# Cross attention: x behind it turned by VectorE and passed through DRAM, its linear one slot later and behind the queries

## The chip, the cores and the metric

One core of one Trainium2 chip runs the whole program. The metric is the time of one execution on the device in microseconds (us), lower is better. Engines are called TensorE (PE; its loads of weights PEld), VectorE (DVE), ScalarE (ACT), GpSimd (POOL) and SyncE (SP), as in the profile.

## The reference

Two transformer layers on x of 4 x 1024 x 512 in float32. The first layer is a state-space mixer, a cross attention and a tanh of three linears; the second is a windowed attention, a strided cross attention and a feed-forward on 4-bit values. Each is added to x and normalised. The stage that matters here is the middle of the first layer:

```python
qh = (q @ Wq.T + bq).reshape(B, S, H, D_K).transpose(0, 2, 1, 3)
scores = jnp.einsum('bhqd,bhkd->bhqk', qh, kh) / np.sqrt(D_K)
scores = jnp.where(mask, scores, -1000000000.0)
weights = jax.nn.softmax(scores, axis=-1)
out = jnp.einsum('bhqk,bhkd->bhqd', weights, vh)
...
return out @ Wo.T + bo                  # x = layernorm(x + this)
...
h = jnp.einsum('btc,cd->btd', x, weight)
h = jnp.einsum('btc,cd->btd', h, aux_weight1)
h = jnp.einsum('btc,cd->btd', h, aux_weight2)
return jnp.tanh(h + bias)               # x = layernorm(x + this)
```

There are 16 heads of 32 and 64 keys. The three linears have no non-linearity between them and are folded to one matrix `WF` in the stage before; keys and values are laid out there too (`KBD`, `VBD`).

## The kernel before

Five stages run one after the other: constants, the mixer with products of weights, `cross_attention_and_linears` (the one that changes), local attention, and the rest with the feed-forward. x stays in SBUF all the time, as 32 tiles of 128 tokens by 512 (`NT = 32`); tile n is of batch n % 4 and group n // 4.

The stage is a software pipeline written out by hand. Every engine walks the same list of slots, `SLOTS`, from -8 on, and in slot s does its part for several tiles; engines meet only by semaphores, each engine doing its own list strictly in order. In slot s TensorE does, in this order: transposes of x of tile s + 8 (`transpose_x`, four, L954), transposes of the softmax weights of tile s - 2 (`transpose_p`, eight, L994), a `query` product for four tiles at a time (L977, a product a slot, so until slot 27), `weigh` of tile s - 2 (L1002, weights times values), transposes of the normalised x2 of tile s - 3 (`transpose_x2`, four, again L954), `scores` of tile s (L986), `project` of tile s - 2 (L1012) and `linear` of tile s - 3 (L1022). In float32 each 128x512 matmul stands as two instructions in the trace.

VectorE does in slot s: `biased` (the linear's product plus its bias, L1131), `total` of the last slot's exponentials and their reciprocal (L1102, L1105), `added` (x plus the tanh, and its statistics, L1136), `masked` (scores times the mask, out of PSUM, L1090), the normalisation of the layer behind (L1119), `shifted` (maximum and subtraction, L1096 and L1098), `attended` (x plus the projection, L1125, and its statistics) and its normalisation. Between `masked` and `shifted` GpSimd adds the mask's fill (`hide`, L921). ScalarE copies the transposes out of PSUM (L1052, L1057, L1074, L1079), evicts the query (L1069), and does exp (L1082) and tanh (L1061). GpSimd also scales by the reciprocals (L926), adds a bias to x (L932) and takes the inverse roots (L939, L948).

The three products of a slot share two PSUM banks in turn:

```python
turn = lambda n, i: 5 + (3 * n + i) % 2
```

So a product may start only when the product two before it has been taken out of its bank. Before the change the order is query, project, linear: `query` follows on the bank of the last slot's `project` and waits for its sum, `s_a2`, i.e. `attended`; `project` follows on the last slot's `linear` and waits for `s_lbd`, i.e. `biased`; `linear` follows on this slot's `query` and waits for `s_qe`.

Of the kernel before, what the change touches and what calls it, by code (L numbers as in the profile page):

```python
# [13 lines left out]
P = 128  # L14
B = 4
# [43 lines left out]
class Kernel:  # L59
    def __init__(self, nc, ctx, a, out):  # L60
# [18 lines left out]
        self.GTd, self.AOd = self.dram("unit_gT", (B * C, P, T)), self.dram("attended", (P, B * C, T))  # L79
        self.YD = self.dram("half_log_norm", (B, 3 * H, T), BF16)  # L80
# [769 lines left out]
def cross_attention_and_linears(k):  # L850
# [6 lines left out]
    with ExitStack() as ctx:  # L857
# [26 lines left out]

        turn = lambda n, i: 5 + (3 * n + i) % 2
# [4 lines left out]
        SLOTS = range(-2 * B, NT + 5)  # L890

        with k.nc.Block() as block:
            @block.sync
            def _(e):
# [3 lines left out]
                for t, n in ((bo, "L0_xattn_bo"), (lb, "L0_ffn_bias")):  # L898
                    e.dma_start(t[:, :], rows_of(a[n])).then_inc(s_lb.sem, 16)

# [4 lines left out]
                e.dma_start(bg[:, :], rows_of(a["L1_attn_bg"])).then_inc(s_next.sem, 16)  # L905
                e.wait_ge(s_next.sem, s_next.at(48))

            @block.gpsimd
            def _(e):
# [24 lines left out]
                for s in SLOTS:  # L934
                    if there(s - 1):
                        weights(s - 1)
                    if there(s - 4):
                        e.wait_ge(s_v3.sem, s_v3.at(s - 3))
                        e.tensor_tensor(rs3[:, :], ve3[:, :], k.mhalf[:, 0:1], ALU.pow).then_inc(s_r3.sem, 1)  # L939
# [11 lines left out]
            def _(e):  # L951
# [5 lines left out]
                def transpose_x(n):  # L957
                    e.wait_ge(s_xe.sem, s_xe.at(n - 11))
# [4 lines left out]
                def transpose_x2(n):  # L963
                    e.wait_ge(s_x2.sem, s_x2.at(n + 1))
                    e.wait_ge(s_tc.sem, s_tc.at(min(n + 12, NT)))
                    e.wait_ge(s_xe.sem, s_xe.at(n))
                    transposed(XTB, x_tile(n), s_xl)

                def query(i):
# [5 lines left out]
                    e.wait_ge(s_a2.sem, s_a2.at(s - 2))  # L975
# [30 lines left out]
                def project(n):  # L1006
# [3 lines left out]
                    e.wait_ge(s_lbd.sem, s_lbd.at(n - 1))  # L1010
                    for c in range(C):
                        mm = e.matmul(bank[turn(s, 1)][:, :], AT[:, c, :], WoT[:, c, :], start=(c == 0), stop=(c == C - 1))  # L1012
                    mm.then_inc(s_o.sem, 1)

                def linear(n):
                    s = n + 3
                    e.wait_ge(s_xe.sem, s_xe.at(n + 1))

                    e.wait_ge(s_qe.sem, s_qe.at(min(s + B + 1, NT)))
                    e.wait_ge(s_a2.sem, s_a2.at(min(n, NT)))  # L1020
                    for c in range(C):
                        mm = e.matmul(bank[turn(s, 2)][:, :], XL[:, c, :], WF[:, c, :], start=(c == 0), stop=(c == C - 1))  # L1022
                    mm.then_inc(s_l.sem, 1)

                for s in SLOTS:
# [4 lines left out]
                    if there(s + B):  # L1030
                        query(s + B)
                    if there(s - 2):
                        weigh(s - 2)
                    if there(s - 3):
# [5 lines left out]
                    if there(s - 3):  # L1040
                        linear(s - 3)

            @block.scalar
            def _(e):
                four = lambda x: x.rearrange("p (n t) -> p n t", n=C)

                for s in SLOTS:
# [10 lines left out]
                    if there(s - 4):  # L1058
                        n = s - 4
                        e.wait_ge(s_lbd.sem, s_lbd.at(n + 1))  # L1060
                        e.activation(TH[:, :], TH[:, :], ACT.Tanh).then_inc(s_th.sem, 1)  # L1061
# [13 lines left out]
                    if there(s - 3):  # L1075
                        n = s - 3
                        e.wait_ge(s_xl.sem, s_xl.at(n + 1))
                        e.wait_ge(s_l.sem, s_l.at(n))
                        e.activation(XL[:, :, :], four(bank[XTB][:, :]), ACT.Copy).then_inc(s_xe.sem, 1)  # L1079
                    if there(s):  # L1080
                        e.wait_ge(s_sx.sem, s_sx.at(s + 1))
                        e.activation(SM[s % RS][:, :], SM[s % RS][:, :], ACT.Exp).then_inc(s_e.sem, 1)  # L1082

            @block.vector
            def _(e):
# [35 lines left out]
                def attended(n):  # L1121
# [3 lines left out]
                    e.tensor_tensor(y, bank[turn(n + 2, 1)][:, :], y, ALU.add).then_inc(s_a2.sem, 1)  # L1125
                    statistics(n, y, st2, mv2, ve2, s_a2, s_t2, s_m2, s_v2, s_r2)

                def biased(n):
                    e.wait_ge(s_l.sem, s_l.at(n + 1))
                    e.wait_ge(s_a3.sem, s_a3.at(n))  # L1130
                    e.tensor_tensor(TH[:, :], bank[turn(n + 3, 2)][:, :], lb[:, :], ALU.add).then_inc(s_lbd.sem, 1)  # L1131
# [6 lines left out]

                e.wait_ge(s_bq.sem, s_bq.at(16))
                e.tensor_scalar(bqs[:, :], bq[:, :], SC, None, ALU.mult).then_inc(s_bqs.sem, 1)  # L1140
                e.wait_ge(s_lb.sem, s_lb.at(32))
                for s in SLOTS:
                    if there(s - 4):
                        biased(s - 4)
                    if there(s - 1):
                        total(s - 1)
                    if there(s - 4):
# [1374 lines left out]
```

## Time and profile before

| | us |
|---|---|
| median of the runs shown | 2681.29 (2680.92 to 2684.01) |
| the profiled execution | 2683.64 |
| its span, first to last instruction | 2681.8 |
| mean granted clock of TensorE | 0.988 |
| TensorE, VectorE, GpSimd, ScalarE busy | 2556.6, 1915.6, 866.7, 749.1 |
| this stage's first `masked` to its last instruction | 420.3 to 906.7 |

In the profile a row of the timeline has the start, the duration, the engine, the line, the operation and in brackets the idle time before it with what ended it. Matmuls one behind the other are merged to one row with their count. "PEclk" is the granted share of TensorE's clock, 1.00 being 2.4 GHz and 0.50 being 1.2 GHz. Issues of DMAs stand under the queue that issues them (SPq, ACTq).

### The profile page before, as it was taken

Reading aid. Unit: us, or ns where it says so; the run is one execution under the profiler, and the core shown is the slowest. Engines: PE = TensorE matmul, PEld = TensorE weight load, DVE = VectorE, ACT = ScalarE, POOL = GpSimd, SP = SyncE. Lnnn points to the kernel's source line nnn. Section 1 sums busy time; section 2 is a strip of 40 time slices with the busy share of each in tenths; the row PEclk is TensorE's granted clock in tenths of the full one; section 3 lists DMA queues with packets and bytes.
Section 4 is the critical chain, followed back from the end, with each engine's and each line's share of the span. In section 5 each row is a group of like instructions: output and inputs, shape, how many; then the busy total and the mean of one; then the engine's idle time right before and its main releaser. Section 6 shows DMA issues by size and latency. Waiting matters only on the chain. (4 is left out here: it accounts for less than half of the span.)

```text
span 2681.8 us, 36822 instructions
## 1 busy us (share of the span) xinstructions
PE 2556.6 (95%) x13053; PEld 1575.2 (59%) x13053; DVE 1915.6 (71%) x3262; ACT 749.1 (28%) x1103; POOL 866.7 (32%) x900
## 2 busy tenths in 40 slices
PE   8999998999999898999988879999999999999998
PEld 4444544555555444454544447777777777777775
DVE  4788403666667436777778858888888888888886
ACT  1111223333332235666668621111110111111100
POOL 2222203555455346676767711111111111111000
PEclk9999999999999999999999979999999999999999
DMA  5444130000000143343444421111111111111111
GB/s 175 146 151 171 52 98 35 1 0 1 1 1 1 33 103 98 98 103 95 106 105 134 139 95 36 45 45 45 46 46 44 46 43 43 43 43 46 38 39 36
DMA packets 269604, 175.94 MB, mean 66 GB/s; under 512 B 104912, under 2 KB 235344, under 8 KB 268399
## 3 DMA queue, kind: packets, MB, share of 16 engines
q1 hardware_dynamic: 238742, 148.59, 19.3%
q10 hardware_dynamic: 30680, 24.98, 3.3%
q8 instruction: 107, 1.75, 0.3%
q14 instruction: 75, 0.61, 0.1%
HBM read 90.51 MB, written 52.43 MB: 53 GB/s over the span
## 5 line engine op out<-in xcount | busy, mean ns | idle before, releaser
L2099 PE MATMUL bank<-tiles,tl_XQT 128*128 128x512 f32 (+1 forms) x768 | 328.1, 570 | 0.8 <-issue 0.8
L2104 PE MATMUL bank<-tiles,tl_XQT 128*128 128x512 f32 (+1 forms) x768 | 317.9, 557 | 0.0
L2116 PE MATMUL bank<-tiles,tl_HT 128*128 128x512 f32 x682 | 304.2, 602 | 5.0 <-DMA tl_HT<-tl_tmp 5.0
L2099 PEld LDWEIGHTS bank<-tiles,tl_XQT 128*128 128x128 f32 x768 | 233.5, 310 | 72.6 <-issue 15.8
L2104 PEld LDWEIGHTS bank<-tiles,tl_XQT 128*128 128x128 f32 x768 | 236.7, 308 | 65.9 <-issue 0.5
L2116 PEld LDWEIGHTS bank<-tiles,tl_HT 128*128 128x128 f32 x682 | 219.2, 324 | 75.7 <-issue 10.9
L1403 POOL TENSOR_SCALAR_AFFINE_SELECT tiles<-tiles 128x512 f32<-128x512 f32 x256 | 182.7, 716 | 170.1 <-ACT tiles L1630 154.4
L2179 ACT ACTIVATE tl_HQ<-bank 128x512 f32<-128x512 f32 (+1 forms) x96 | 53.9, 562 | 580.4 <-PE bank L2099 545.7
L2046 POOL TENSOR_TENSOR tl_rs<-tl_ve,mhalf 128x1 f32<-128x1 f32 x29 | 15.9, 548 | 537.1 <-DVE tl_ve L2258 537.1
L1730 DVE SCALAR_TENSOR_TENSOR tiles<-tiles,bank 128x1024 f32<-128x1024 f32 (+1 forms) x128 | 141.7, 1148 | 18.8 <-PE bank L1506 18.7
L1408 POOL TENSOR_SCALAR_AFFINE_SELECT tiles<-tiles 128x512 f32<-128x512 f32 x224 | 152.6, 681 | 0.0
L2038 POOL TENSOR_TENSOR tl_rs<-tl_ve,mhalf 128x1 f32<-128x1 f32 x32 | 18.7, 584 | 402.0 <-DVE tl_ve L2240 402.0
L1630 ACT ACTIVATE tiles<-bank 128x1024 f32<-128x1024 f32 (+1 forms) x128 | 123.4, 964 | 28.2 <-PE bank L1465 28.1
L1635 ACT ACTIVATE tiles<-tiles 128x1024 f32<-128x1024 f32 (+1 forms) x128 | 124.8, 1000 | 20.0 <-DVE tiles L1730 17.0
L1555 PE MATMUL bank<-home_T,tiles 128*128 128x512 f32 x256 | 121.5, 619 | 3.5 <-ACT tiles L1664 0.9
L977 PE MATMUL bank<-space_T 128*128 128x512 f32 x256 | 118.6, 607 | 2.5 <-DVE X L1125 2.3
L1567 PE MATMUL bank<-home_odd,tiles 128*128 128x512 f32 x256 | 117.4, 601 | 0.0
L1022 PE MATMUL bank<-space_T,space_quant 128*128 128x512 f32 x256 | 115.2, 593 | 1.5 <-ACT space_quant L1079 1.5
L1012 PE MATMUL bank<-space_even,space_quant 128*128 128x512 f32 x256 | 115.3, 593 | 1.2 <-ACT space_quant L1074 1.1
L1428 POOL TENSOR_TENSOR la_rn<-la_n,mhalf 128x16 f32<-128x16 f32 x32 | 92.7, 2897 | 52.2 <-DVE la_n L1805 52.2
L2054 PE MATMUL bank<-home_T,attended_values 128*128 128x512 f32 x232 | 107.1, 605 | 0.0
L921 POOL TENSOR_TENSOR xl_SM<-xl_SM,xl_nm 128x1024 f32<-128x1024 f32 x32 | 80.0, 2499 | 78.8 <-DVE xl_SM L1090 78.8
(301 smaller groups left out, 4701.3 us busy)
## 6 DMA issues: line engine op xcount, KB each, us to landing
tl_HT<-tl_tmp SPq DMA_DIRECT2D x248, 44.0 KB, 2.0
tl_HT<-tl_tmp ACTq DMA_DIRECT2D x248, 44.0 KB, 2.0
fp_weights<-space_quant ACTq DMA_DIRECT2D x33, 256.0 KB, 2.5
X<-in_x SPq DMA_DIRECT2D x8, 1024.0 KB, 10.7
v<-tiles SPq DMA_DIRECT2D x32, 256.0 KB, 2.4
unit_g<-tiles SPq DMA_DIRECT2D x32, 256.0 KB, 2.4
unit_gT<-tiles SPq DMA_DIRECT2D x128, 64.0 KB, 2.1
la_GN<-unit_g SPq DMA_DIRECT2D x128, 64.0 KB, 2.0
```

The costliest lines, as they stand in the source:

```text
L977: mm = e.matmul(bank[turn(s, 0)][:, :], WqT[:, c, m * P:(m + 1) * P], XT[g % 2][:, c, :], start=(c == 0), stop=(c == C - 1))
L1012: mm = e.matmul(bank[turn(s, 1)][:, :], AT[:, c, :], WoT[:, c, :], start=(c == 0), stop=(c == C - 1))
L1403: return e.affine_select(out=x[:, :, 0:P], in_=x[:, :, 0:P], compare_op=ALU.is_ge, fill=fill, base=0, pattern=[[0, HC], [1, P]], channel_m ...
L1408: return e.affine_select(out=x[:, :, P:WIN], in_=x[:, :, P:WIN], compare_op=ALU.is_ge, fill=fill, base=0, pattern=[[0, HC], [-1, P]], chan ...
L1555: mm = e.matmul(bank[1][:, :], XT[m % 2][:, c, :], WgT[:, c, :], start=(c == 0), stop=(c == C - 1))
L1567: mm = e.matmul(bank[2][:, :], XT[m % 2][:, c, :], WvT[:, c, :], start=(c == 0), stop=(c == C - 1))
L1630: e.activation(TR[p % RING][:, :, 0:cols(t)], four(ARG[:, :])[:, :, 0:cols(t)], ACT.Tanh).then_inc(s_T.sem, 1)
L1635: e.activation(y, y, ACT.Exp).then_inc(s_p.sem, 1)
L1730: e.scalar_tensor_tensor(out=y, in0=y, scalar=1.0, in1=d, op0=ALU.add, op1=ALU.mult).then_inc(s_u.sem, 1)
L2099: mm = e.matmul(bank[(2 * q) % 3][:, 0:w], chunk(XQT[n % 2], c), WgT[q][:, :, c, :], start=(c == 0), stop=(c == C - 1))
L2104: mm = e.matmul(bank[(2 * q + 1) % 3][:, 0:w], chunk(XQT[n % 2], c), WuT[q][:, :, c, :], start=(c == 0), stop=(c == C - 1))
L2116: mm = e.matmul(bank[DOWN][:, :], chunk(HT, q), WdT[:, q, :], start=(q == 0), stop=(q == IC - 1))
```

## The change

The x2 that the linear reads is no longer turned by TensorE and copied out by ScalarE. VectorE turns it in blocks of 32x32 into one of two new tiles, `XB2`, behind the normalisation (`x2_turned`). In the next slot SyncE stores the four quarters of it to DRAM in four DMAs, each putting its blocks in place, and ScalarE's queue loads the whole back in one DMA, into the tile `XL`, whose columns now lie token by token with the four chunks side by side. The last two tiles keep TensorE's transposes. The `linear` of a tile runs one slot later than before, and within its slot behind `query` instead of at the end; `biased` stays with the same tile's slot number s - 4 but moves behind `shifted`, `added` and its normalisation go one slot later, and tanh moves behind exp. The order of the three products in the shared banks is now query, linear, project, and each waits accordingly: `query` for `biased` of the slot before, `linear` for `attended` of the slot before, `project` for this slot's `query`. There is one slot more at the end.

```diff
+        self.X2d = self.dram("x2_turned", (2, P, D))
...
-        SLOTS = range(-2 * B, NT + 5)
+        SLOTS = range(-2 * B, NT + 6)
...
+        by_blocks = lambda n: 0 <= n < NT - 2
+        XB2 = [sb(f"XB2{n}", [P, D]) for n in range(2)]
+        XLT = XL[:, :, :].rearrange("p c t -> p (c t)")
+        in_chunks = lambda x: x.rearrange("p (t c) -> p c t", c=C)
+        s_tu, d_tu, d_xl = sem("x2_turned"), [sem(f"x2_stored{n}") for n in range(2)], sem("x2T_load")
...
+                def x2_stored(n):
+                    e.wait_ge(s_tu.sem, s_tu.at(n + 1))
+                    e.wait_ge(d_xl.sem, d_xl.at(16 * (n - 1)))
+                    for i in range(4):
+                        e.dma_start(k.X2d[n % 2].rearrange("(j p) w -> p j w", j=4)[:, :, P * i:P * i + P],
+                                    XB2[n % 2][32 * i:32 * i + 32, :].rearrange("p (j w) -> p j w", j=4)).then_inc(d_tu[n % 2].sem, 16)
...
+                for s in SLOTS:
+                    if by_blocks(s - 3):
+                        x2_stored(s - 3)
...
-                    if there(s - 4):
-                        e.wait_ge(s_v3.sem, s_v3.at(s - 3))
+                    if there(s - 5):
+                        e.wait_ge(s_v3.sem, s_v3.at(s - 4))
                         e.tensor_tensor(rs3[:, :], ve3[:, :], k.mhalf[:, 0:1], ALU.pow).then_inc(s_r3.sem, 1)
...
                 def transpose_x(n):
-                    e.wait_ge(s_xe.sem, s_xe.at(n - 11))
                     if n > B:
...
                 def transpose_x2(n):
                     e.wait_ge(s_x2.sem, s_x2.at(n + 1))
-                    e.wait_ge(s_tc.sem, s_tc.at(min(n + 12, NT)))
-                    e.wait_ge(s_xe.sem, s_xe.at(n))
+                    e.wait_ge(s_tc.sem, s_tc.at(NT))
+                    e.wait_ge(s_xe.sem, s_xe.at(n - NT + 2))
                     transposed(XTB, x_tile(n), s_xl)
...
                     s = i - B
                     e.wait_ge(s_qe.sem, s_qe.at(i - 1))
-                    e.wait_ge(s_a2.sem, s_a2.at(s - 2))
+                    e.wait_ge(s_lbd.sem, s_lbd.at(s - 4))
...
                     s = n + 2
                     e.wait_ge(s_ae.sem, s_ae.at(n + 1))
 
+                    e.wait_ge(s_qe.sem, s_qe.at(min(s + B + 1, NT)))
+                    e.wait_ge(s_lbd.sem, s_lbd.at(n - 2))
+                    for c in range(C):
+                        mm = e.matmul(bank[turn(s, 2)][:, :], AT[:, c, :], WoT[:, c, :], start=(c == 0), stop=(c == C - 1))
+                    mm.then_inc(s_o.sem, 1)
+                def linear(n):
+                    s = n + 4
+                    if by_blocks(n):
+                        e.wait_ge(d_xl.sem, d_xl.at(16 * (n + 1)))
+                    else:
+                        e.wait_ge(s_xe.sem, s_xe.at(n - NT + 3))
+                    e.wait_ge(s_a2.sem, s_a2.at(min(s - 2, NT)))
                     e.wait_ge(s_lbd.sem, s_lbd.at(n - 1))
                     for c in range(C):
-                        mm = e.matmul(bank[turn(s, 1)][:, :], AT[:, c, :], WoT[:, c, :], start=(c == 0), stop=(c == C - 1))
-                    mm.then_inc(s_o.sem, 1)
-
-                def linear(n):
-                    s = n + 3
-                    e.wait_ge(s_xe.sem, s_xe.at(n + 1))
-
-                    e.wait_ge(s_qe.sem, s_qe.at(min(s + B + 1, NT)))
-                    e.wait_ge(s_a2.sem, s_a2.at(min(n, NT)))
-                    for c in range(C):
-                        mm = e.matmul(bank[turn(s, 2)][:, :], XL[:, c, :], WF[:, c, :], start=(c == 0), stop=(c == C - 1))
+                        mm = e.matmul(bank[turn(s, 1)][:, :], in_chunks(XLT)[:, c, :], WF[:, c, :], start=(c == 0), stop=(c == C - 1))
                     mm.then_inc(s_l.sem, 1)
 
                 for s in SLOTS:
@@ -1029,16 +1053,16 @@
                         transpose_p(s - 2)
                     if there(s + B):
                         query(s + B)
+                    if there(s - 4):
+                        linear(s - 4)
                     if there(s - 2):
                         weigh(s - 2)
-                    if there(s - 3):
+                    if there(s - 3) and not by_blocks(s - 3):
                         transpose_x2(s - 3)
                     if there(s):
                         scores(s)
                     if there(s - 2):
                         project(s - 2)
-                    if there(s - 3):
-                        linear(s - 3)
 
             @block.scalar
             def _(e):
@@ -1055,10 +1079,6 @@
                         e.wait_ge(s_pt.sem, s_pt.at(n + 1))
                         e.wait_ge(s_at.sem, s_at.at(n))
                         e.activation(PT[:, :, :], PTB.rearrange("p (n t) -> p n t", n=H // 2), ACT.Copy).then_inc(s_pe.sem, 1)
-                    if there(s - 4):
-                        n = s - 4
-                        e.wait_ge(s_lbd.sem, s_lbd.at(n + 1))
-                        e.activation(TH[:, :], TH[:, :], ACT.Tanh).then_inc(s_th.sem, 1)
                     if there(s + B):
                         i = s + B
                         g, m = i // C, i % C
@@ -1072,14 +1092,23 @@
                         e.wait_ge(s_at.sem, s_at.at(n + 1))
                         e.wait_ge(s_o.sem, s_o.at(n))
                         e.activation(AT[:, :, :], four(bank[AB][:, :]), ACT.Copy).then_inc(s_ae.sem, 1)
-                    if there(s - 3):
+                    if by_blocks(s - 3):
                         n = s - 3
-                        e.wait_ge(s_xl.sem, s_xl.at(n + 1))
+                        e.wait_ge(d_tu[n % 2].sem, d_tu[n % 2].at(64 * (n // 2 + 1)))
                         e.wait_ge(s_l.sem, s_l.at(n))
-                        e.activation(XL[:, :, :], four(bank[XTB][:, :]), ACT.Copy).then_inc(s_xe.sem, 1)
+                        e.dma_start(XLT, k.X2d[n % 2]).then_inc(d_xl.sem, 16)
+                    elif there(s - 3):
+                        n = s - 3
+                        e.wait_ge(s_xl.sem, s_xl.at(n - NT + 3))
+                        e.wait_ge(s_l.sem, s_l.at(n))
+                        e.activation(in_chunks(XLT), four(bank[XTB][:, :]), ACT.Copy).then_inc(s_xe.sem, 1)
                     if there(s):
                         e.wait_ge(s_sx.sem, s_sx.at(s + 1))
                         e.activation(SM[s % RS][:, :], SM[s % RS][:, :], ACT.Exp).then_inc(s_e.sem, 1)
+                    if there(s - 4):
+                        n = s - 4
+                        e.wait_ge(s_lbd.sem, s_lbd.at(n + 1))
+                        e.activation(TH[:, :], TH[:, :], ACT.Tanh).then_inc(s_th.sem, 1)
 
             @block.vector
             def _(e):
@@ -1122,13 +1151,13 @@
                     y = x_tile(n)
                     e.wait_ge(s_o.sem, s_o.at(n + 1))
                     e.wait_ge(s_xb.sem, s_xb.at(n + 1))
-                    e.tensor_tensor(y, bank[turn(n + 2, 1)][:, :], y, ALU.add).then_inc(s_a2.sem, 1)
+                    e.tensor_tensor(y, bank[turn(n + 2, 2)][:, :], y, ALU.add).then_inc(s_a2.sem, 1)
                     statistics(n, y, st2, mv2, ve2, s_a2, s_t2, s_m2, s_v2, s_r2)
 
                 def biased(n):
                     e.wait_ge(s_l.sem, s_l.at(n + 1))
                     e.wait_ge(s_a3.sem, s_a3.at(n))
-                    e.tensor_tensor(TH[:, :], bank[turn(n + 3, 2)][:, :], lb[:, :], ALU.add).then_inc(s_lbd.sem, 1)
+                    e.tensor_tensor(TH[:, :], bank[turn(n + 4, 1)][:, :], lb[:, :], ALU.add).then_inc(s_lbd.sem, 1)
 
                 def added(n):
                     y = x_tile(n)
@@ -1136,25 +1165,32 @@
                     e.tensor_tensor(y, TH[:, :], y, ALU.add).then_inc(s_a3.sem, 1)
                     statistics(n, y, st3, mv3, ve3, s_a3, s_t3, s_m3, s_v3, s_r3)
 
+                def x2_turned(n):
+                    e.wait_ge(s_x2.sem, s_x2.at(n + 1))
+                    e.wait_ge(d_tu[n % 2].sem, d_tu[n % 2].at(64 * (n // 2)))
+                    e.transpose(XB2[n % 2][:, :].rearrange("p (j r c) -> p c j r", j=4, r=32), x_tile(n)).then_inc(s_tu.sem, 1)
                 e.wait_ge(s_bq.sem, s_bq.at(16))
                 e.tensor_scalar(bqs[:, :], bq[:, :], SC, None, ALU.mult).then_inc(s_bqs.sem, 1)
                 e.wait_ge(s_lb.sem, s_lb.at(32))
                 for s in SLOTS:
+                    if there(s - 1):
+                        total(s - 1)
+                    if there(s - 5):
+                        added(s - 5)
+                    if there(s):
+                        masked(s)
+                    if there(s - 5):
+                        normal(s - 5, mv3, rs3, s_r3, s_x3)
+                    if there(s):
+                        shifted(s)
                     if there(s - 4):
                         biased(s - 4)
-                    if there(s - 1):
-                        total(s - 1)
-                    if there(s - 4):
-                        added(s - 4)
-                    if there(s):
-                        masked(s)
-                    if there(s - 4):
-                        normal(s - 4, mv3, rs3, s_r3, s_x3)
-                    if there(s):
-                        shifted(s)
                     if there(s - 2):
                         attended(s - 2)
                         normal(s - 2, mv2, rs2, s_r2, s_x2)
+                    if by_blocks(s - 2):
+                        x2_turned(s - 2)
 
 
 FULL = P + 1
```

## Rows read from the trace of the kernel before

**Rows 1.** The page's part 1: busy us and share of the span, instructions.
```profile
PE 2556.6 (95%) x13053; PEld 1575.2 (59%) x13053; DVE 1915.6 (71%) x3262; ACT 749.1 (28%) x1103; POOL 866.7 (32%) x900
```

**Rows 2.** Windows, a stretch mid-stage: us, busy of each engine, PEclk, DMA share, GB/s.
```profile
634.00:691.00 57.00, 57.00 (x244) 32.70 (x241) 36.68 (x61) 19.01 (x27) 29.59 (x22) 1.00 0.00 1
```

**Rows 3.** Timeline of one steady slot: start us, us, engine, line, operation, count, [idle before].
```profile
651.51 3.60 PE L1012 MATMUL bank<-space_even,space_quant 128*128 128x512 f32 x8
...
651.72 1.23 DVE L1090 TENSOR_TENSOR xl_SM<-bank,xl_mf 128x1024 f32<-128x1024 f32 x1 [1.93 <-PE bank L986]
...
654.95 3.60 PE L1022 MATMUL bank<-space_T,space_quant 128*128 128x512 f32 x8
...
658.03 0.68 DVE L1125 TENSOR_TENSOR X<-bank,X 128x512 f32<-128x512 f32 x1
...
658.38 0.60 PE L954 MATMUL bank<-ident,X 128*128 128x128 f32 x4
...
659.69 3.60 PE L977 MATMUL bank<-space_T 128*128 128x512 f32 x8
...
663.22 1.09 PE L1002 MATMUL bank<-xl_PT,space_quant 128*64 128x128 f32 x16
...
664.25 0.66 PE L954 MATMUL bank<-ident,X 128*128 128x128 f32 x4
...
664.74 1.89 PE L986 MATMUL bank<-space_quant,space_T 128*128 128x256 f32 x8
...
666.67 1.23 DVE L1090 TENSOR_TENSOR xl_SM<-bank,xl_mf 128x1024 f32<-128x1024 f32 x1 [1.91 <-PE bank L986]
```

**Rows 4.** Timeline of the third slot.
```profile
445.27 1.04 PE L994 MATMUL bank<-ident,xl_SM 128*128 128x128 f32 x8
...
447.75 0.68 DVE L1125 TENSOR_TENSOR X<-bank,X 128x512 f32<-128x512 f32 x1
...
448.58 5.37 PE L977 MATMUL bank<-space_T 128*128 128x512 f32 x8 [2.27 <-DVE X L1125]
...
449.30 1.02 ACT L1057 ACTIVATE xl_PT<-bank 128x1024 f32<-128x1024 f32 x1
...
457.32 1.23 DVE L1090 TENSOR_TENSOR xl_SM<-bank,xl_mf 128x1024 f32<-128x1024 f32 x1 [5.11 <-PE bank L986]
```

**Rows 5.** Line L1090 in slots 26 and 27: op, count, ns min/median/max, starts.
```profile
L1090 DVE TENSOR_TENSOR xl_SM<-bank,xl_mf x2: 1224/1224/1225, 799.9 to 814.4; 128x1024 f32<-128x1024 f32 x2
```

**Rows 6.** Timeline: the last `masked`, and the stage's last VectorE instruction.
```profile
867.07 1.23 DVE L1090 TENSOR_TENSOR xl_SM<-bank,xl_mf 128x1024 f32<-128x1024 f32 x1
...
906.10 0.55 DVE L1119 TENSOR_SCALAR X<-X,xl_mv,xl_rs 128x512 f32<-128x512 f32 x1 [0.66 <-POOL xl_rs L939]
```

**Rows 7.** Windows of 2 us behind the waits of rows 4 and 8.
```profile
450.00:452.00 2.00, 2.00 (x4) 0.93 (x3) 1.71 (x3) 0.32 (x1) 0.21 (x1) 0.50 0.00 0
850.00:852.00 2.00, 2.00 (x14) 1.67 (x12) 1.97 (x4) 1.17 (x3) 0.00 (x1) 0.50 0.00 0
874.00:876.00 2.00, 0.45 (x9) 0.41 (x10) 1.17 (x4) 1.54 (x2) 0.43 (x1) 1.00 0.00 0
```

**Rows 8.** Timeline of TensorE: two waits of the last slots.
```profile
849.01 1.85 PE L1002 MATMUL bank<-xl_PT,space_quant 128*64 128x128 f32 x16 [1.92 <-ACT xl_PT L1057]
...
873.01 1.04 PE L994 MATMUL bank<-ident,xl_SM 128*128 128x128 f32 x8
...
875.60 1.09 PE L1002 MATMUL bank<-xl_PT,space_quant 128*64 128x128 f32 x16 [1.55 <-ACT xl_PT L1057]
```

**Rows 9.** Line L2381, a transpose on VectorE: count, ns min/median/max, starts.
```profile
L2381 DVE STREAM_TRANSPOSE tl_QB<-tl_XQ x31: 1082/1109/1166, 1594.2 to 2618.8; 128x512 f32<-128x512 f32 x31
```

**Rows 10.** The page's part 6: DMA issues, count, KB each, us to landing.
```profile
tl_HT<-tl_tmp SPq DMA_DIRECT2D x248, 44.0 KB, 2.0
...
fp_weights<-space_quant ACTq DMA_DIRECT2D x33, 256.0 KB, 2.5
X<-in_x SPq DMA_DIRECT2D x8, 1024.0 KB, 10.7
```

## The prediction

> **What bounds the kernel now.** I read the page's busy times first: TensorE works 95% of the span [rows 1], so a change pays only where it shortens TensorE's stream or its waits. The windows of the stage come next: in the middle of the cross attention TensorE is busy for all of 57 us, while VectorE has 36.68 and ScalarE 19.01 [rows 2]. The time order of one slot then gives the order that the stage lives by [rows 3]. I count a slot from one `masked` (VectorE, L1090) to the next: 651.72 to 666.67, 14.95 us. The reader should see two things. VectorE, which runs `masked` to the end of `attended`'s sum (658.03 + 0.68 = 658.71), holds a PSUM bank that the next `query` needs; `query` starts at 659.69, so today this comes 0.83 us early, allowing the 0.15 us that lay between such a sum's end and the query elsewhere (448.43 to 448.58 [rows 4]). And it comes early only because TensorE has two products of 3.44 us, `project` and `linear`, to do between `scores` and `query`.
>
> The same time order at the third slot [rows 4] is the one place where that cover is missing: there is no `linear` yet, and `query` waits 2.27 us for the sum of L1125. The whole argument rests on this row.
>
> **The change, part by part.** *Removed:* four transposes of x2 per tile, 30 times. From L954's start at 664.25 to `scores` at 664.74 is 0.49 us [rows 3]. A TensorE that never waited would need 14.95 - 0.49 = 14.46 us a slot. The copy on ScalarE goes too, worth nothing, since ScalarE has a third of the work.
>
> *Moved:* `linear`, one slot later, from behind `project` to behind `query`. Its bank is now emptied by `biased`, which VectorE reaches only behind `masked` and `shifted` of that slot; and `query` of the next slot waits for exactly that `biased` (`s_lbd.at(s - 4)`). Now only `project` and twelve transposes lie between `scores` and `query`, as in rows 4. So a ring closes: scores, masked, hide on GpSimd, max, subtraction, biased, query, linear, weigh, scores. It is worked out with steady rows:
> - `masked` to the end of the sum, which `biased` replaces at the same shape: 651.72 to 658.71, 6.99 us [rows 3]; `hide` on GpSimd is inside it.
> - to `query`: 0.15 us [rows 4].
> - `query` to `weigh`, today adjacent: 659.69 to 663.22, 3.53 us; `linear` between them adds 651.51 to 654.95, 3.44 us [rows 3].
> - `weigh` to what follows it: 663.22 to 664.25, 1.03 us; `scores` to `masked`: 664.74 to 666.67, 1.93 us [rows 3].
>
> Sum 17.07 us a slot. Behind the waiting `query` stand linear, weigh, scores and project, in that order, so everything waits. TensorE would stand still 17.07 - 14.46 = 2.6 us in each slot.
>
> Which slots? `query` is there up to slot 27 and its wait means something from slot 5 on. Step by step:
> - *Slots 3 and 4 gain.* `query` of slot 3 no longer waits for `attended`. It would start near 446.3, when the eight transposes of P end (445.27 + 1.04 [rows 4]); `weigh` then waits for the copy of P^T (449.30 + 1.02 = 450.32 [rows 4]) and starts at 450.45, so masked(3) is at 450.45 + 1.03 + 1.93 = 453.4 instead of 457.32. masked(4) follows 14.46 later, at 467.9, instead of 457.32 + 14.95 = 472.3. Gain 4.4 us.
> - *Slots 5 to 27:* 23 x 17.07 = 392.6, so masked(27) at 860.5 instead of 814.4 [rows 5]: 46.1 us late.
> - *Slots 28 to 31* have no `query`. There `linear` waits for `attended`, which is one sum further on (0.68 + 0.03): 6.99 + 0.71 + 0.15 + 3.53 + 1.03 + 1.93 = 14.34 a slot, 57.4 in all, so masked(31) at 917.9 instead of 867.07 [rows 6]: 50.8 us late.
> - *The drain* from masked(31) to the stage's last instruction takes 906.10 + 0.55 - 867.07 = 39.6 us [rows 6]. One slot is added, but the slots are short there. Following VectorE through slots 32 to 36 with the same durations I get 41.6: 2.0 more.
>
> Sum 52.8 us without any effect on the clock.
>
> *The clock.* Where TensorE waited 2.27 us, the clock then fell to 0.50, which is the 1.2 GHz level (450 to 452 [rows 7]), and the query took 5.37 instead of 3.60 us, 1.77 more [rows 3, 4]. After a wait of 1.92 us it fell too, after one of 1.55 us it did not [rows 7, 8]. Here each of 27 slots has such a wait, of 2.6 us or more. From below this costs 0, from above 27 x 1.77 = 48 us. I take one in three for the 23 waits of 2.6 us, nearer to never, since they are only a little above the one that cost nothing, and all four in slots 28 to 31, where a sum more (0.71) comes before `linear` and four transposes fewer before the wait, so that it is about 3.5 us: 12 x 1.77 = 21 us.
>
> There is a rule that bears on this. The Trainium skill, page "TensorE: Matmul & The Clock Gate", section "Part 4: PE-mode transpose", says that transposes do not count as activity for the clock the way matmuls do. By that rule the twelve transposes and the wait behind them would be one long pause, and the clock would fall in every slot. The trace bears it out only by half: after eight transposes and 1.55 us of waiting the clock was still at 1.00 [rows 7, 8]. It is rival 2 below.
>
> *Added on VectorE:* 30 transposes of 128x512, 1.11 us each at the nearest row, which also writes with a stride [rows 9]. VectorE stands idle 1.91 us before `masked` now [rows 3], so its own round is 14.95 - 1.91 = 13.04, and becomes 14.2 us. That lies beside a ring of 17.07: nothing. If the cover went (TensorE at 14.46) it would still just fit; in slots 28 to 31 it equals the ring, and I count nothing.
>
> *Added DMAs:* four stores of 64 KB on SP's queue, one load of 256 KB on ScalarE's. A transfer out of a turned tile lands after 2.0 us, a 256 KB one after 2.5 [rows 10]; the upper bound is 10.7 us, that of 1 MB. SP has only the next stage's weights ahead of them, issued at the stage's start. The turned tile is ready at the latest when VectorE's round ends, 14.2 us after `masked`; four stores one after another, 2.0 each, are there by 22.2, and the load behind them by 24.7. ScalarE is free for it before that: it gets there behind `weigh` of the next slot, at 17.07 - 1.93 = 15.1 and a copy. `linear` needs it two slots on, at 34.14 - 1.93 - 1.03 - 3.53 = 27.7. Three us of slack by upper bounds: nothing. Behind the issue on ScalarE stand exp and tanh; exp of that slot waits for `shifted` anyway, until 17.07 + 6.3 = 23.4, so a load issued by then holds up nothing.
>
> *Other edits at nothing:* tanh behind exp (its reader `added` is a slot's start later); `transpose_x` without its wait; the stationary operand read in steps of four elements, since a load of weights has a 512-column product to hide behind. The later `added` costs only the drain, counted above.
>
> **The sum.** 52.8 + 21 = 74 us on the profiled execution of 2683.6, whose span is 2681.8. That execution is 2.35 above the median of the runs, 2681.3, so I forecast 2755.
>
> **The rivals.**
> 1. *The ring without the clock.* For it: between waits TensorE works ten us and more at a stretch, and 1.55 us did no harm. Against: two of two longer ones did. 2681.3 + 52.8 = 2734.
> 2. *The clock falls in every slot.* 2681.3 + 52.8 + 48 = 2782. For it: the row of rows 4 is the same order of work. Against: a fall lengthens the slot, so the next wait meets other work before it.
> 3. *The bank is free in time and TensorE stays the bound* (the other side). This holds from the point where masked-to-biased takes less than project and twelve transposes, 3.44 + 1.31 (658.38 to 659.69 [rows 3]) = 4.75 instead of 7.1 us. Then -4.4, 19 slots at 14.46 and 4 at 14.0 (no more x to turn ahead) against 342.1 give -15.7 by slot 27, VectorE's 14.2 in the last four gives +4.6, the drain +2: -9, so 2672. Against: all durations on that path are measured, and none of its instructions goes.
> 4. *The transfers are late.* If stores and load took 10.7 us each, the turned x would be there at 14.2 + 10.7 + 10.7 = 35.6 instead of 27.7, 7.9 late over two slots, so 4 a slot: 23 x 4 = 92 more than the forecast, 2847. Against: this stage leaves the DMA engines idle (their share is 0.00 in [rows 2]).
>
> **How the numbers follow.** Forecast, the ring with a clock that falls in some slots: 0.58. Rival 1: 0.18. Rival 2: 0.16. Rival 3: 0.05. Rival 4: 0.03. The range takes in the first three with a few us for a ring that is 0.2 us a slot shorter or longer: 2729 to 2789. About 0.2% (5 us) is what a measurement can tell from no change. Faster is rival 3, 0.05; same 0.02, a partial form of it; slower 0.93.
>
> **What would show it.** In the changed trace: `masked` to `masked` near 17.1 us or 18.8, not 14.95; TensorE waiting some 2.5 us before `query`, released by VectorE's `biased`, 23 times; the granted clock at 0.50 after some of these; no wait at `linear` for the load; VectorE still idle before `masked`. I am wrong if `query` starts straight behind the transposes of P, or if `linear` waits for a DMA.

## The result: slower by 2.5%, by a ring through the queries' bank

| | before | changed |
|---|---|---|
| median, us | 2681.51 | 2750.16 (2749.24 to 2753.03) |
| ratio | | 1.0254, 95% interval 1.0239 to 1.0268 |
| span of the profiled execution | 2681.8 | 2749.3 |
| last instruction of the stage on VectorE ends at | 906.65 | 974.22 |

The ratios here and below are of fast runs alone; one execution of e6 (9374.67 us) and one of the kernel before beside it (10908.97 us) are slow ones and are left out.

The forecast was 2755. The stage ends 67.6 us later, the span is 67.5 longer, so all of it is in this stage. On the page TensorE's busy time has hardly moved against [rows 1] (2556.6), only its share of a longer span; and the group of the queries (line, shapes, count, busy and mean ns, then the idle time before them and what ended it) names the loss:

```profile
PE 2557.7 (93%) x12933; PEld 1595.3 (58%) x12933; DVE 1944.9 (71%) x3292; ACT 728.0 (26%) x1073; POOL 866.3 (32%) x900
...
L997 PE MATMUL bank<-space_T 128*128 128x512 f32 x256 | 123.6, 628 | 57.7 <-DVE xl_TH L1160 57.7
```

One steady slot of the changed kernel in order of time, to be laid beside [rows 3]:

```profile
643.77 1.23 DVE L1119 TENSOR_TENSOR xl_SM<-bank,xl_mf 128x1024 f32<-128x1024 f32 x1 [3.17 <-PE bank L1006]
...
650.09 0.68 DVE L1160 TENSOR_TENSOR xl_TH<-bank,xl_lb 128x512 f32<-128x512 f32 x1
...
650.91 3.67 PE L997 MATMUL bank<-space_T 128*128 128x512 f32 x8 [2.44 <-DVE xl_TH L1160]
...
653.75 1.11 DVE L1171 STREAM_TRANSPOSE xl_XB<-X 128x512 f32<-128x512 f32 x1
...
654.42 3.60 PE L1046 MATMUL bank<-space_T,space_quant 128*128 128x512 f32 x8
...
657.95 1.09 PE L1022 MATMUL bank<-xl_PT,space_quant 128*64 128x128 f32 x16
...
658.98 1.99 PE L1006 MATMUL bank<-space_quant,space_T 128*128 128x256 f32 x8
...
661.01 1.23 DVE L1119 TENSOR_TENSOR xl_SM<-bank,xl_mf 128x1024 f32<-128x1024 f32 x1 [3.18 <-PE bank L1006]
```

The reader should see the ring closing: `masked` (L1119) at 643.77, `biased` (L1160) behind `shifted`, `query` (L997) 0.14 us after `biased` ends and 2.44 us late, then `linear`, `weigh`, `scores`, and `masked` again at 661.01: 17.24 us, against 14.95. VectorE is no bound, since it idles 3.18 us before `masked`.

### The profile page after: what moved, and what is told of

Its sections match the earlier page's. It is cut to its first block and busy times, and to the rows that moved or that the text cites. A ratio compares the mean times of both kernels' runs of the same rounds, so it can differ in the third digit from the quotient of the medians.

```text
span 2749.3 us, 36735 instructions
## 1 busy us (share of the span) xinstructions
PE 2557.7 (93%) x12933; PEld 1595.3 (58%) x12933; DVE 1944.9 (71%) x3292; ACT 728.0 (26%) x1073; POOL 866.3 (32%) x900
## 5 line engine op out<-in xcount | busy, mean ns | idle before, releaser
L997 PE MATMUL bank<-space_T 128*128 128x512 f32 x256 | 123.6, 628 | 57.7 <-DVE xl_TH L1160 57.7
L1046 PE MATMUL bank<-space_T,space_quant 128*128 128x512 f32 x256 | 121.8, 620 | 19.1 <-issue 18.0
L1119 DVE TENSOR_TENSOR xl_SM<-bank,xl_mf 128x1024 f32<-128x1024 f32 x32 | 39.1, 1223 | 112.6 <-PE bank L1006 112.6
L997 PEld LDWEIGHTS bank<-space_T 128*128 128x128 f32 x256 | 48.5, 200 | 112.4 <-issue 112.1
```

Of the source, the lines that this page charges most:

```text
L997: mm = e.matmul(bank[turn(s, 0)][:, :], WqT[:, c, m * P:(m + 1) * P], XT[g % 2][:, c, :], start=(c == 0), stop=(c == C - 1))
L1046: mm = e.matmul(bank[turn(s, 1)][:, :], in_chunks(XLT)[:, c, :], WF[:, c, :], start=(c == 0), stop=(c == C - 1))
```

## The experiments

Each run shows the edit against the changed kernel. Line numbers in the text are the changed kernel's; in the rows they are those of the run. "A slot" is from one `masked` to the next; its number is that of the tile that `masked` then takes, and slots are measured from the starts of that line in the profiled execution. "The drain" is from the last `masked`, masked(31), to the stage's last instruction on VectorE. "A fall" is a stretch in which the granted clock of TensorE is 0.50 (1.2 GHz) instead of 1.00. "VectorE's round" is the time from one `masked` to the next when `masked` does not wait for `scores`: VectorE's own work and its waits for GpSimd. Rival A holds VectorE's transposes to be the cost, rival B the passage through DRAM.

**e1, `biased` ahead of `masked`.**

```diff
                     if there(s - 5):
                         added(s - 5)
+                    if there(s - 4):
+                        biased(s - 4)
                     if there(s):
                         masked(s)
...
-                    if there(s - 4):
-                        biased(s - 4)
```

> The changed kernel with one thing put back: VectorE takes `biased` of tile s - 4 ahead of `masked` instead of behind `shifted`. Theory (the ring through `biased`): `query` finds its bank empty, the wait of 2.44 us before it goes 23 times, a slot is TensorE's own stream, 14.5 us instead of 17.24, and the whole kernel comes to 2674 us (2670 to 2680), below the kernel before. Rival A (VectorE's transposes are the cost): a slot stays above 15 us, 2690 or more, and VectorE has no idle time before `masked`. Rival B (the passage through DRAM is late): `linear` waits instead of `query`, and the time stays near 2750.

Measured 2682.97, ratio to the kernel before 0.9996 (0.9987 to 1.0005): no difference from before, and 67 us below the changed kernel. In the timeline of e1 the query follows the transposes without a wait:

```profile
642.68 1.22 DVE L1119 TENSOR_TENSOR xl_SM<-bank,xl_mf 128x1024 f32<-128x1024 f32 x1 [0.47 <-PE bank L1006]
...
646.35 1.04 PE L1014 MATMUL bank<-ident,xl_SM 128*128 128x128 f32 x8
...
647.23 3.60 PE L997 MATMUL bank<-space_T 128*128 128x512 f32 x8
...
657.25 1.22 DVE L1119 TENSOR_TENSOR xl_SM<-bank,xl_mf 128x1024 f32<-128x1024 f32 x1 [0.44 <-PE bank L1006]
```

A slot is 14.56 us and masked(27) comes at 801.1, 13.3 us earlier than in the kernel before. So the cause is shown: this one position costs the whole loss. But I had forecast 2674, and 11.9 of the 13.3 us were lost again behind it: slots 28 to 31 took 61.8 us (before: 52.6) and the drain 42.3 (39.6). In slot 29, where the clock did not fall, the slot is 13.99 us, VectorE's round; the other three are 15.45, 15.57 and 16.83, so of the 9.2 us lost there 5.9 are falls. The profiled execution is the slowest of the eleven of e1 (2684.69; the fastest, 2674.71, had a mean granted clock of 0.989 instead of 0.985), so not every execution loses as much. `linear` waits for `attended` in these slots, by its semaphore and by the times (L1154 ends 0.11 us before it), and the clock falls behind the wait:

```profile
852.43 0.68 DVE L1154 TENSOR_TENSOR X<-bank,X 128x512 f32<-128x512 f32 x1
853.22 6.75 PE L1046 MATMUL bank<-space_T,space_quant 128*128 128x512 f32 x8 [2.83 <-issue]
```

**e2, the order alone,** x2 turned by TensorE and copied by ScalarE as before.

```diff
-        by_blocks = lambda n: 0 <= n < NT - 2
+        by_blocks = lambda n: False
...
                 def transpose_x(n):
+                    e.wait_ge(s_xe.sem, s_xe.at(n - 11))
...
-                    e.wait_ge(s_tc.sem, s_tc.at(NT))
-                    e.wait_ge(s_xe.sem, s_xe.at(n - NT + 2))
+                    e.wait_ge(s_tc.sem, s_tc.at(min(n + 12, NT)))
+                    e.wait_ge(s_xe.sem, s_xe.at(n))
...
```

> The changed kernel's order on all engines, but x2 turned by TensorE and copied by ScalarE for all tiles, with no transpose on VectorE and no new DMA. Theory (the ring): the loss is all there, and the four transposes between `weigh` and `scores` lie inside the ring: 17.24 + 0.49 = 17.73 us a slot, 2763 us in all (2755 to 2785, by how often the clock falls). Rivals A and B (VectorE's transposes, the passage through DRAM): without them the time comes back to 2681 or at least below 2700.

Measured 2773.75, ratio 1.0338 (1.0324 to 1.0352). The loss is there without a transpose on VectorE or a new DMA, so rivals A and B are out. Two queries in the timeline of e2 show the same wait as above and a slot of 17.63 us. That is 0.1 less than the 17.73 expected: with the transposes of x2 ahead of it again, `scores` to `masked` takes 1.93 us (612.75 to 614.68) and not the changed kernel's 2.03:

```profile
604.20 3.67 PE L998 MATMUL bank<-space_T 128*128 128x512 f32 x8 [2.45 <-DVE xl_TH L1161]
...
621.83 3.67 PE L998 MATMUL bank<-space_T 128*128 128x512 f32 x8 [2.44 <-DVE xl_TH L1161]
```

It is slower than my 2763 because the clock fell in 9 of slots 5 to 27 (5, 8, 11 and so on to 26, and 27); more on that below.

**e3, the turning alone,** with the products in the old order (query, project, linear).

```diff
                 def query(i):
-                    e.wait_ge(s_lbd.sem, s_lbd.at(s - 4))
+                    e.wait_ge(s_a2.sem, s_a2.at(s - 2))
...
-                    if there(s - 4):
-                        linear(s - 4)
                     if there(s - 2):
                         weigh(s - 2)
...
                         project(s - 2)
+                    if there(s - 4):
+                        linear(s - 4)
...
                 for s in SLOTS:
+                    if there(s - 5):
+                        biased(s - 5)
                     if there(s - 1):
                         total(s - 1)
```

> The other half alone: x2 turned by VectorE and passed through DRAM, its linear one slot later, but the products in the order of the kernel before (query, project, linear at the slot's end) with its waits, `biased` at the head of VectorE's slot, tanh where it was; the load stands behind exp on ScalarE's queue. Theory (the ring): two products lie again between `scores` and `query`, which waits for `attended` and finds it done; 14.5 us a slot while x is still turned ahead, 14.1 to 14.3 in the last slots where VectorE's round bounds: 2676 us (2671 to 2682). Rivals A and B: 2700 and more, since everything that they blame is in it.

Measured 2683.63, ratio 1.0003 (0.9994 to 1.0012). The rivals' "2700 and more" is wrong, the ring's middle is right (14.56 us a slot), and my 2676 is too low for the same reason as in e1: from its first `masked` to masked(27) it is 10.7 us faster than before, but the last four slots take 56.5 us, 14.12 each, which is VectorE's round with the transpose, and the drain 47.0, since `linear` is a slot later and at that slot's end. I had booked next to nothing for either.

**e4, no transpose, no store, no load.** `x2_turned`, `x2_stored` and the load are not called, nor waited for.

> The changed kernel without VectorE's 30 transposes, the 120 stores and the 30 loads; the linear of tiles 0 to 29 multiplies whatever lies in its tile, so the values of x are not the reference's from there on, the work of all other instructions being the same. Theory (the ring): none of them is in the ring, a slot stays 17.24 us and the time 2750 (2740 to 2758). Rivals A and B: the time falls by 30 us or more.

Measured 2753.97, ratio 1.0264 (1.0249 to 1.0278), as the ring has it. The wait in its timeline is the same:

```profile
641.83 1.23 DVE L1114 TENSOR_TENSOR xl_SM<-bank,xl_mf 128x1024 f32<-128x1024 f32 x1 [4.20 <-PE bank L1005]
...
648.98 3.67 PE L996 MATMUL bank<-space_T 128*128 128x512 f32 x8 [2.44 <-DVE xl_TH L1155]
...
659.07 1.23 DVE L1114 TENSOR_TENSOR xl_SM<-bank,xl_mf 128x1024 f32<-128x1024 f32 x1 [4.20 <-PE bank L1005]
```

The slot is 17.24 and VectorE's idle time before `masked` grows by 1.03 us, from 3.17 to 4.20: in slots 5 to 27 the transpose had lain in it. In the last four slots e4 is no clean comparison: they took 67.4 us, 6.1 more than in the changed kernel, since behind nearly the same wait as there (3.38 us, 3.43 in the changed kernel) the clock stayed low for longer and `linear` took 6.45 us instead of 3.60:

```profile
891.41 6.45 PE L1043 MATMUL bank<-space_T,space_quant 128*128 128x512 f32 x8 [3.38 <-DVE X L1149]
```

**e5, the ring cut at the fill.**

```diff
                     e.wait_ge(s_mk.sem, s_mk.at(n + 1))
-                    e.tensor_tensor(x, x, nm[(n // B) % 2][:, n % B, :].unsqueeze(1).to_broadcast([P, H, S2]), ALU.add).then_inc(s_hid.sem, 1)
+                    e.wait_ge(s_hid.sem, s_hid.at(n))
+                    e.memset(none[:, :], 0.0).then_inc(s_hid.sem, 1)
...
                 def shifted(n):
-                    e.wait_ge(s_hid.sem, s_hid.at(n + 1))
+                    e.wait_ge(s_mk.sem, s_mk.at(n + 1))
```

> The changed kernel with the ring cut at another member: GpSimd no longer adds the mask's fill (`hide` is a memset of one column), and `shifted` waits for `masked` alone; masked scores are 0 and not -1e9, so the values differ from the reference's. The fill takes the time between the layer normalisation behind `masked` and the maximum, 645.45 to 647.69 in the changed kernel's steady slot, 2.2 us. Theory (the ring): a slot is 17.24 - 2.2 = 15.04, some 0.5 us above TensorE's own 14.56, the wait before `query` shrinks from 2.44 to 0.3, the clock no longer falls there, and the whole comes to 2685 us (2678 to 2693). Rival (the ring is not what bounds, GpSimd's fill being hidden): 2745 or more.

Measured 2671.98, ratio to the kernel before 0.9963 (0.9949 to 0.9977), 78 us below the changed kernel. In the timeline of e5 a slot is 14.91 us (15.04 expected), and TensorE is ready for the query almost when `biased` ends:

```profile
639.55 1.23 DVE L1120 TENSOR_TENSOR xl_SM<-bank,xl_mf 128x1024 f32<-128x1024 f32 x1 [3.18 <-PE bank L1007]
...
643.53 0.69 DVE L1161 TENSOR_TENSOR xl_TH<-bank,xl_lb 128x512 f32<-128x512 f32 x1
...
644.37 3.67 PE L998 MATMUL bank<-space_T 128*128 128x512 f32 x8
...
654.46 1.23 DVE L1120 TENSOR_TENSOR xl_SM<-bank,xl_mf 128x1024 f32<-128x1024 f32 x1 [3.17 <-PE bank L1007]
```

`masked` to the end of `biased` is 4.67 us (639.55 to 644.22), 7.00 in the changed kernel: 2.33 us out of the ring took 2.33 us off the slot. The total is below my 2685 because I left out the other slots. From the first `masked` to masked(4) e5 takes 4.4 us less than the changed kernel, slots 28 to 31, at 12.15 and without falls, 12.7 less, and the drain 3.8 less.

**e7 and e8, each transpose done twice,** in the changed kernel and in e1.

```diff
+                    e.transpose(XB2[n % 2][:, :].rearrange("p (j r c) -> p c j r", j=4, r=32), x_tile(n)).then_inc(s_once.sem, 1)
+                    e.wait_ge(s_once.sem, s_once.at(n + 1))
                     e.transpose(XB2[n % 2][:, :].rearrange("p (j r c) -> p c j r", j=4, r=32), x_tile(n)).then_inc(s_tu.sem, 1)
```

> The changed kernel with each of VectorE's 30 transposes done twice, 1.11 us more a slot. Theory (the ring): VectorE has 3.17 us of idle time before `masked`, so slots stay at 17.24; only the last four, at 14.48 against a round of VectorE of 14.1, could grow by 0.8 each: 2752 us (2742 to 2760). Rival A (VectorE's transposes are the cost): 30 x 1.11 = 33 more, 2783.

> The same doubling in the kernel with `biased` ahead of `masked` (e1), where a slot is 14.56 us and VectorE's idle time before `masked` 0.4. Here the cover is gone: VectorE's round of 14.1 becomes 15.25, so slots 5 to 27 grow to 15.25 and the last by 1.1: 23 x 0.7 + 4 x 1.1 = 20 more, 2703 us (2697 to 2712). If it stays at 2683, VectorE's round is shorter than I read it.

Measured 2756.5 (ratio 1.0278, 1.0261 to 1.0294) and 2700.65 (1.0070, 1.0055 to 1.0084). The same 33 us of VectorE cost some 6 us in the one, 18 in the other. In e7 the slot without a fall is still 17.24; slots 5 to 27 take 4.5 us more than in the changed kernel only by three more falls, and slots 28 to 31 2.4 more. In e8 a slot is 15.17 and `masked` no longer waits. First e7, where the 3.76 of the first row stands behind a fall and the 2.04 of the second is the steady value, then e8:

```profile
643.75 1.23 DVE L1120 TENSOR_TENSOR xl_SM<-bank,xl_mf 128x1024 f32<-128x1024 f32 x1 [3.76 <-PE bank L1007]
...
660.98 1.23 DVE L1120 TENSOR_TENSOR xl_SM<-bank,xl_mf 128x1024 f32<-128x1024 f32 x1 [2.04 <-PE bank L1007]
```

```profile
650.09 1.21 DVE L1120 TENSOR_TENSOR xl_SM<-bank,xl_mf 128x1024 f32<-128x1024 f32 x1
...
665.26 1.22 DVE L1120 TENSOR_TENSOR xl_SM<-bank,xl_mf 128x1024 f32<-128x1024 f32 x1
```

**e6, e9 and e10, the last slots mended in e1.** e6 and e9 are one kernel; e10 is the same with `LATE = 2`.

```diff
+        LATE = 6
-        by_blocks = lambda n: 0 <= n < NT - 2
+        by_blocks = lambda n: 0 <= n < NT - LATE
+        line_bank = lambda s: turn(s, 1) if s < NT - B else 5
+        proj_bank = lambda s: turn(s, 2) if s < NT - B else 6
...
                 def linear(n):
-                    e.wait_ge(s_a2.sem, s_a2.at(min(s - 2, NT)))
-                    e.wait_ge(s_lbd.sem, s_lbd.at(n - 1))
+                    if s < NT - B:
+                        e.wait_ge(s_a2.sem, s_a2.at(s - 2))
+                        e.wait_ge(s_lbd.sem, s_lbd.at(n - 1))
+                    else:
+                        e.wait_ge(s_lbd.sem, s_lbd.at(n))
```

(`project` waits for `s_a2` of tile n - 1 from slot 28 on.)

> The kernel with `biased` ahead of `masked` (e1), with two changes for its last slots, where it lost again what it had won: only tiles 0 to 25 are turned by VectorE and the last six by TensorE, and from slot 28 on, where there is no query, `linear` and `project` keep a bank each, so that neither waits for `attended` of the slot before. Theory (the last slots are bound by VectorE's round, 14.1 us with the transpose and 13.0 without, and by waits of TensorE that let the clock fall): slots 28 to 31 take 52 to 54 us instead of 61.8, the stage ends near 895 and the whole is 2673 us (2668 to 2679). Rival (the last slots are bound by TensorE and the added slot alone): no change, 2683.

> The kernel e6 once more, word for word, for a better interval of its difference from the kernel before: 2672 us (2669 to 2675), ratio 0.996.

> e6 with one of its two changes only: `linear` and `project` keep a bank each from slot 28 on, but tiles 0 to 29 are turned by VectorE as in the changed kernel. Theory (two causes in the last slots: the waits for `attended`, and VectorE's round of 14.1 with its transpose): slots 28 to 31 take 4 x 14.1 = 56.5 us, between e1's 61.8 and e6's 54.0, and the whole 2675 us (2672 to 2679). If only the waits matter it equals e6; if only VectorE's round matters it equals e1, 2683.

Measured: e6 2671.74 (without the execution left out above), ratio 0.9959 (0.9945 to 0.9973); e9 2671.87, 0.9954 (0.9940 to 0.9968); e10 2674.15, 0.9965 (0.9953 to 0.9978). All three are faster than both kernels, e9 by 0.46% than the one before: little, but no interval reaches 1. In e9's timeline slots 30 and 31 are 12.98 and 12.97 us (13.59 and 12.99 in the kernel before), and VectorE does not wait at their ends:

```profile
828.57 1.23 DVE L1127 TENSOR_TENSOR xl_SM<-bank,xl_mf 128x1024 f32<-128x1024 f32 x1 [0.99 <-PE bank L1009]
...
841.55 1.21 DVE L1127 TENSOR_TENSOR xl_SM<-bank,xl_mf 128x1024 f32<-128x1024 f32 x1
...
854.52 1.22 DVE L1127 TENSOR_TENSOR xl_SM<-bank,xl_mf 128x1024 f32<-128x1024 f32 x1
```

Slots 28 to 31 take 54.0 us in e6 and e9 and 56.0 in e10 (61.8 in e1). Most of what e1 lost there came back by the banks alone. A slot of e10 is 14.00 us, no shorter than e1's slot without a fall; what is gone are e1's 5.9 us of falls. The clock still falls in e10's last slots (0.50 at 826 to 828), but no slot is longer for it. The six tiles left to TensorE bring 2 us more by the profiles, but the whole times of e9 and e10 have intervals that overlap, so that part is not shown by them.

**e11, the changed kernel again,** with no edit.

> The changed kernel once more, to see whether the number of times that the clock falls is its own or that of one execution: the slot without a fall is 17.24 again, and by my forecast's share of one in three the clock falls in 8 of slots 5 to 27; in its first profile it was 3. If it is 2 to 4 again, the share is set by how the slots lie in time and not by the length of the wait, which is the same in e2 (8 of 23).

Measured 2753.87 in two runs, ratio 1.0264 (1.0245 to 1.0283). The clock fell in 3 of slots 5 to 27 again (5, 9 and 18; the first time 5, 9 and 19).

## Why the prediction was right

Direction and mechanism held, and the size nearly: 68.6 us by the medians against a forecast of 74, with one term, the clock, taken twice too large. By its own steps:

- *Slots 3 and 4 gain 4.4 us.* Measured 4.1 (masked(4) at 468.16, 472.27 before). `query` at 446.32, `weigh` at 450.54 released by the copy of P^T, masked(3) at 453.60: forecast 446.3, 450.45 and 453.4.

```profile
446.32 3.60 PE L997 MATMUL bank<-space_T 128*128 128x512 f32 x8
450.54 1.09 PE L1022 MATMUL bank<-xl_PT,space_quant 128*64 128x128 f32 x16 [0.63 <-ACT xl_PT L1081]
453.60 1.23 DVE L1119 TENSOR_TENSOR xl_SM<-bank,xl_mf 128x1024 f32<-128x1024 f32 x1 [0.18 <-PE bank L1006]
```

- *The ring, 17.07 us.* Measured 17.24, so 4 us more over 23 slots. Of the 0.17, 0.10 is in scores to masked: 658.98 to 661.01 is 2.03, where I took 1.93 from a slot in which transposes stood ahead of `scores` (e2, which has them there, shows 1.93 again); 0.07 is in query to linear, 3.51 instead of 3.44. e1, e2 and e5 change three different members, and the slot follows each.
- *Slots 28 to 31, 14.34 each, and the wait for `attended` there.* The two slots without a fall are 14.47 and 14.48, the others 16.17 and 16.18:

```profile
885.74 1.23 DVE L1119 TENSOR_TENSOR xl_SM<-bank,xl_mf 128x1024 f32<-128x1024 f32 x1 [2.13 <-PE bank L1006]
...
893.43 3.79 PE L1046 MATMUL bank<-space_T,space_quant 128*128 128x512 f32 x8 [3.43 <-issue]
...
900.21 1.22 DVE L1119 TENSOR_TENSOR xl_SM<-bank,xl_mf 128x1024 f32<-128x1024 f32 x1 [0.42 <-PE bank L1006]
```

- *The drain, 41.6.* Measured 974.22 - 930.87 = 43.35, with one fall of the clock in it, worth 1.7.
- *VectorE's transposes and the DMAs at nothing.* Right in slots 5 to 27: 1.11 us each as in [rows 9], and e4 shows them free there; in the last four no run parts them from the clock. The stores landed after 1.8 us and the load after 2.6 (median), against 2.0 and 2.5 taken from [rows 10]. e8 shows what the transposes cost with the cover gone, and the last slots of e3 and e1 that it was gone there.
- *The clock, 21 us: the term that was mis-sized.* The forecast was a fall in 8 of slots 5 to 27 and in all of the last four, 12 x 1.77. Measured: 3 and 2, at 1.70 and 1.69 each, and the one in the drain: 10 us. The waits behind which it fell are as long as those behind which it did not. This is the one of slot 9; the query takes 5.37 us, and 3.67 in the slot after, behind the same wait:

```profile
545.78 5.37 PE L997 MATMUL bank<-space_T 128*128 128x512 f32 x8 [2.45 <-DVE xl_TH L1160]
```

```profile
564.72 3.67 PE L997 MATMUL bank<-space_T 128*128 128x512 f32 x8 [2.44 <-DVE xl_TH L1160]
```

```profile
548.00:550.00 2.00, 2.00 (x4) 0.97 (x3) 1.92 (x3) 0.04 (x1) 0.01 (x1) 0.50 0.00 0
642.00:644.00 2.00, 2.00 (x10) 1.55 (x9) 0.23 (x1) 0.45 (x1) 0.00 (x0) 1.00 0.45 129
```

The last fence has windows of 2 us with the granted clock in the third column from the end: 0.50 (1.2 GHz) during that query, 1.00 (2.4 GHz) mid-stage. I had taken the length of the wait as what decides. With that wait at 2.44 us (2.87 in slots 24 to 27, where no x is turned ahead any more) the clock fell in 2 (e4), 3, 3 (e11) and 6 (e7) of the 23 slots of 17.24 us, and in 9 of those of 17.63 us in e2. In slots 24 to 27 it fell four times in e7 and never in the changed kernel, behind the same wait. So the share is no property of the wait alone. The falls do not lie at random: in slots of 17.24 us they come nine or ten slots apart once the first are past (9 and 19; 9 and 18 in e11; 10 and 20 in e4; 5, 14 and then 24 to 27 in e7), in e2's of 17.63 us every third. So it matters when the waits come and not only how long they are; what sets this order no run tests. My one in three had no row behind it either: in the rows of before, both waits above 1.9 us were followed by a fall and only the one of 1.55 was not, and 2.6 lies above all three. That the sum came within 7 us is in part luck.

Rival 2, by which twelve transposes and the wait would be one long pause and the clock fall in every slot, is not borne out: by that reading of the Trainium skill's rule ("TensorE: Matmul & The Clock Gate", "Part 4: PE-mode transpose") there would have been 23 falls, and there were 3. That refutes a fall in every slot; whether transposes count for the clock, these runs do not settle.

The errors had opposite signs: clock -11, ring and last slots about +5, slots 3 and 4 +0.3.

Rival 3, by which the kernel would have gained 9 us, tells what the change lacked. It needed the bank free in time, and e1 is that kernel: by slot 27 it gains 13.3 us, where that rival said 15.7. My price for its last slots was too low, 4.6 us (four slots of 14.2 against 52.6 are in fact 4.2) where 9.2 were lost, because I left out the waits for `attended` and the clock behind them in that branch, though I had them in the main one: 3.3 of the 9.2 are VectorE's round, 5.9 the falls.

## What to carry to other kernels

When a product moves in TensorE's list, look up which bank it now follows and where, in the other engine's list, that bank is emptied: a wait on an instruction that stands behind one which itself waits for TensorE closes a ring, and then the slot is the sum of the ring and no busy time. Such an eviction belongs ahead of the first instruction that waits for TensorE in the same slot. Look at the last slots by themselves: here an edit worth 13 us in the middle was worth nothing in all until they had banks of their own.

## What the runs showed of the hardware

- The granted clock fell to 0.50 behind waits of 2.44 us in some slots and not in others of the same execution, and the second execution of the same kernel had nearly the same slots. One fall cost 1.69 to 1.70 us in the changed kernel. Some were longer: `linear` took 6.75 us instead of 3.60 in slot 31 of e1 and 6.45 in the last slots of e4, behind waits of 2.83 and 3.38 us.
- Loads of weights read in steps of four elements take 308 ns instead of 190 in the trace (`linear`, L1046, against L1022 in the kernel before), and the products built on them are not slower: `linear` to `weigh` is 654.42 to 657.95, 3.53 us, as `query` to `weigh` in [rows 3].
